# Summing products over states on TensorE: two half sums in two tiles instead of one whole sum every second tile

## What is computed

```
def step(h, inp):
    u_t, dt_t, B_t, C_t = inp
    h = jnp.exp(dt_t[..., None] * A) * h + (dt_t * u_t)[..., None] * B_t[:, :, None, :]
    y = jnp.einsum('bkdn,bkn->bkd', h, C_t)
    return (h, y)
```

## Time and profile before

| | |
|---|---|
| median of 3 runs | 13085.13 us |
| profiled execution, its own time | 13084.96 us |
| its span | 13082.8 us |
| mean granted TensorE clock | 0.697 of full speed |
| TensorE (PE) matmuls | 9361.0 us, 72% |
| VectorE (DVE) | 10128.2 us, 77% |
| GpSimd (POOL) | 9739.9 us, 74% |
| ScalarE (ACT) | 7120.1 us, 54% |

### The profile page before, as it was taken

One profiled execution on the slowest core, in us unless ns is written; L12 is line 12 of the kernel. 1 busy time (PEld: TensorE's weight loads), 2 busy tenths in 40 slices (PEclk: granted clock), 3 DMA queues, 4 the chain that ended last, 5 costly groups with the idle time before them and its releaser, 6 DMA issues.

```text
span 13082.8 us, 94515 instructions
## 1 busy us (share of the span) xinstructions
PE 9361.0 (72%) x26432; PEld 2316.8 (18%) x26432; DVE 10128.2 (77%) x5979; ACT 7120.1 (54%) x10802; POOL 9739.9 (74%) x4231
## 2 busy tenths in 40 slices
PE   5866688766886677768777778876678667776665
PEld 1211122111221112212122112211112111221121
DVE  2899967897689978888788876889778997888600
ACT  3655545554465545766466754655446554676324
POOL 1888867887688877877778776789768887788600
PEclk8955578756785567768777777865679557776665
DMA  3656676566655555545664657656665555555410
GB/s 77 142 130 128 129 129 130 134 128 130 134 139 132 126 142 137 123 121 129 148 136 118 122 135 132 135 130 128 132 132 137 129 128 147 131 128 124 100 47 15
DMA packets 1762968, 1627.25 MB, mean 124 GB/s; under 512 B 1304446, under 2 KB 1305760, under 8 KB 1762444
## 3 DMA queue, kind: packets, MB, share of 16 engines
q1 hardware_dynamic: 1762444, 1621.22, 56.1%
HBM read 622.68 MB, written 192.94 MB: 62 GB/s over the span
## 4 chain that ended last, share of the span: by engine, by line
PE 29%; issue 21%; POOL 16%; DVE 16%; ACT 10%; DMA 5%; SPq 3%; DVEq 0%; POOLq 0%; ACTq 0%
POOL pr L1346 10%; DVE ps L1261 7%; DVE hs L1276 7%; PE ps L669 5%; PE ps L821 4%; PE ps L642 3%; POOL dur L1354 3%; PE ps L808 3%; PE ps L799 3%; PE ps L783 2%; ACT dec L1055 2%; POOL us L1337 2%; DMA sd<-y_d 2%; PE ps L686 2%; SPq L550 1%
## 5 line engine op out<-in xcount | busy, mean ns | idle before, releaser
L1346 POOL TENSOR_TENSOR pr<-hs,crep 128x1024 f32<-128x1024 f32 x3072 | 7187.8, 2351 | 2244.3 <-DVE hs L1276 1230.0
L1276 DVE TENSOR_TENSOR_SCAN hs<-dec,carry,ps 128x1024 f32<-128x1024 f32 x1728 | 4054.0, 2346 | 228.8 <-DVE ps L1261 5.4
L1261 DVE TENSOR_TENSOR ps<-ps,dur 128x1024 f32<-128x1024 f32 x2304 | 2794.2, 1213 | 1133.6 <-PE ps L808 927.5
L808 PE MATMUL ps<-sbc,selb 96*128 96x512 bf16 x4608 | 1929.3, 517 | 1754.0 <-DVE hs L1276 1248.3
L1055 ACT ACTIVATE dec<-dtr,ac 128x1024 f32<-128x1024 f32 x2304 | 2611.8, 1136 | 382.7 <-DVE hs L1276 374.6
L821 PE MATMUL ps<-pr,red 128*32 128x512 f32 x12288 | 2421.6, 873 | 105.3 <-POOL pr L1346 95.9
L1354 POOL TENSOR_TENSOR dur<-dur,brep 128x1024 f32<-128x1024 f32 x768 | 1806.0, 2352 | 135.9 <-DVE ps L1261 97.6
L1062 ACT ACTIVATE carry<-hs 128x1 f32<-128x1 f32 x2304 | 457.6, 199 | 2576.3 <-DVE hs L1276 2379.5
L1272 DVE TENSOR_TENSOR_SCAN hs<-ps,carry,dur 128x1024 f32<-128x1024 f32 x576 | 1337.1, 2335 | 264.9 <-POOL dur L1354 116.8
L1276 DVE TENSOR_TENSOR_SCAN hs<-dec,zero,ps 128x1024 f32<-128x1024 f32 x576 | 1351.6, 2346 | 75.4 <-DVE ps L1261 1.5
L642 PE MATMUL ps<-xb,tapw 96*96 96x512 f32 x2304 | 1200.8, 637 | 43.1 <-ACT sd L896 40.7
(11 more groups left out here) (117 smaller groups left out, 7018.1 us busy)
## 6 DMA issues: line engine op xcount, KB each, us to landing
dtr<-de SPq DMA_DIRECT2D x768, 512.0 KB, 7.7
dur<-us SPq DMA_DIRECT2D x768, 512.0 KB, 8.5
crep<-bc_d SPq DMA_DIRECT2D x512, 512.0 KB, 6.3
ust<-u_d SPq DMA_DIRECT2D x256, 384.0 KB, 5.1
y_d<-yst SPq DMA_DIRECT2D x768, 128.0 KB, 4.2
sd<-y_d SPq DMA_DIRECT2D x512, 192.0 KB, 4.6
brep<-bc_d SPq DMA_DIRECT2D x128, 512.0 KB, 7.5
u_d<-sd SPq DMA_DIRECT2D x64, 384.0 KB, 3.1
```

The lines of the kernel that those rows point to most:

```text
L808: mm = pe.matmul(ps[:, SLOT + 2 * (n % RS) + hf, :], selb[:, i % GT // 2, :], sbc[:, w % 2, B * hf:B * (hf + 1)], start=True, stop=True)
L1261: dve.tensor_tensor(slot(n), slot(n), dur[:, 2 * (G % 2) + i % 2, :], ALU.mult).then_inc(bu_v, 1)
L1276: dve.tensor_tensor_scan(hs[:, n % RH, :], dec[:, others(n) % RD, :], slot(n), init, ALU.mult, ALU.add).then_inc(scan_v, 1)
L1346: pool.tensor_tensor(pr[:, n % RP, :], hs[:, n % RH, :], crep[:, q, :], ALU.mult).then_inc(prod_g, 1)
```

## The change

The pair is the same, and so are the matmuls, their operands, strips and number. The half hf = 0 (strips 0 and 1) is now issued in iteration n = 2m+3, one tile earlier than before, and waits for the pair's products; the half hf = 1 (strips 2 and 3) in iteration n = 2m+4, where the whole pair stood before, and signals that the pair is summed. The wait for the collected bank goes with the first half.

```
-            def reduce2(m):
+            def reduce_half(m, hf):
                 w, r = divmod(m, NP)
                 g, q = divmod(r, NQ)
-                pe.wait_ge(prod_g, 2 * m + 2)
-                if q == 0:
-                    after(pe, ye_a, NG * w + g)
-                for hf in range(2):
-                    for j in range(2):
-                        strip = 2 * hf + j
-                        mm = pe.matmul(ps[32 * strip:32 * strip + 32, YB, :], red[:, :],
-                                       pr[:, (2 * m + j) % RP, B * hf:B * (hf + 1)], start=(q == 0), stop=(q == NQ - 1))
-                mm.then_inc(red_p, 1)
+                if hf == 0:
+                    pe.wait_ge(prod_g, 2 * m + 2)
+                    if q == 0:
+                        after(pe, ye_a, NG * w + g)
+                for j in range(2):
+                    strip = 2 * hf + j
+                    mm = pe.matmul(ps[32 * strip:32 * strip + 32, YB, :], red[:, :],
+                                   pr[:, (2 * m + j) % RP, B * hf:B * (hf + 1)], start=(q == 0), stop=(q == NQ - 1))
+                if hf == 1:
+                    mm.then_inc(red_p, 1)
...
-                    if i % 2 == 0 and n >= 4:
-                        reduce2((n - 4) // 2)
+                    if n >= 3:
+                        reduce_half((n - 3) // 2, (n - 3) % 2)
...
-            for m in range(W * NP - 2, W * NP):
-                reduce2(m)
+            for m in range(2 * (W * NP - 2) + 1, 2 * W * NP):
+                reduce_half(m // 2, m % 2)
```

## The result

The changed kernel takes **13291.57 us** (median of 4 runs, 13276.16 to 13303.08), the kernel before beside it 13082.11 us. The ratio is 1.0154, 95% interval 1.0133 to 1.0176: **1.5% slower, +209 us**. Forecast were 13302 us, +217 us. The size came out right, and half of its parts did not, as the stretches show.

What follows compares the result with a forecast made beforehand. No engine was full; VectorE's loop bounds stretches without side work, TensorE leads the chain in post. Terms 48 (no side work) + 73 (post) + 60 (convolution) + 36 (attention) = +217 us on 13085, 13302 us; range 12970 to 13650.

Steps and rivals of the forecast that it cites:

- A half costs what a whole burst does: Sums on TensorE: two strips take as long as four, so 1536 additional bursts cost 1521 to 2872 us of engine time.
- The figure carried on from the Trainium skill: Sums on TensorE: a straight line from the skill's 2.38 makes a half 0.81 of a whole, total about +65 us.
- TensorE's time by stretch: Windows with side work: TensorE busy 95.5 us in post, 83.2 in convolution, 76.7 in attention, at clocks 0.80, 0.93, 0.78.
- the 10300 that were named as a sign: Whole kernel: TensorE's busy time was to come out above 10300 us.
- No side work: hidden, as argued: Windows without side work: added burst covered by VectorE's 3.6 us in plain tiles; 1 us a window, +48 us.
- The 41 us against 32: Ten preparation tiles without side work: ten halves raise TensorE's work to 41 us against 32.3 us of VectorE.
- I cost this at nothing: First half's earlier wait for the copied bank: TensorE idles 0.75 us three times a window, covered by 0.8 us slack.
- GpSimd's products to be there before the fill is done: Plain tiles without side work: the later product is there before the fill is done, so the added burst is hidden.
- Charge the chain with the printed share of TensorE: Stretches with side work: added TensorE time times 48% in post (+73 us), 27% in convolution (+60), 18% in attention (+36).
- Rival 1: Stretches with side work: a fuller TensorE raises its clock and makes the kernel faster, 12980 us; chance 0.20.
- the 0.85 named as break-even: Post stretches: the granted clock, 76.4/90.1, at which the added bursts neither cost nor gain time.
- Rival 3: Preparation and earlier wait stall VectorE, clock doesn't rise: +7 us a window without side work, +736 in all, 13821 us; chance 0.15.

Runs made afterwards that it cites:

- Experiment 5: The change, but the first pair of each group stays whole in its even tile; 13134.95 us against 13071.85 for the kernel before, ratio 1.0045.
- experiment 1: The kernel before, with all pairs whole but issued one tile earlier; 13182.73 us against 13080.74, ratio 1.0078.
- experiment 6: The kernel before, with whole pairs one tile earlier except the first pair of each group, which keeps its even tile; 13087.46 us, ratio 1.0012.
- experiment 2: The kernel before, with each pair in two halves in its even tile, side work between them; 13168.54 us, ratio 1.0069.
- experiment 3: The change, with halves only for pairs 1 to 5, in the preparation tiles, and whole pairs elsewhere; 13107.99 us, ratio 1.0024 to the kernel before.
- experiment 9: The kernel before, plus two-strip bursts adding zero in odd tiles for pairs 1, 2, 3, 5 outside convolution; 13222.59 us against 13072.79, ratio 1.0111.
- experiment 10: The kernel before, with whole pairs 1, 2, 3 and 5 one tile earlier outside convolution, no burst added; 13038.35 us, ratio 0.9978.

## Why the prediction was right, and where not

- **A half costs what a whole burst does: right.** A four-instruction burst takes 1.05 and 1.92 us, an eight-instruction burst 1.07 and 1.94. From its start to the next matmul's, the half holds TensorE 0.98 us (2330.96 to 2331.94) and 1.85 us (2326.06 to 2327.91), the whole 0.99 and 1.87. L821 is busy 3911.7 us; forecast were about 4000. The figure carried on from the Trainium skill ("TensorE: Matmul & The Clock Gate", "Measured speedup vs the span model"), a half at 0.81 of a whole, is not what this chip does between two and four strips. Its +65 us falls with it. One reading behind the step was wrong, though: L799 is no burst of one strip. Its stationary operand is 96 columns wide (6*96), so that its 2.02 us compare a wide matmul with four narrow ones; only the halves themselves show the price of two strips.
- **TensorE's time by stretch: right.** Post 94.1 us a window ((16 x 98.5 + 12 x 88.3)/28) for 95.5; convolution 84.6 for 83.2; attention 73.3 for 76.7. Clocks 0.80 and 0.84, 0.92, 0.80 for 0.80, 0.93, 0.78. TensorE's busy time in all is 10105.3 us, less than the 10300 that were named as a sign: the sums take 1490 us more and TensorE as a whole only 744, since the rest of its work got shorter at the higher clock (a fill's matmul 466 ns on average instead of 517).
- **No side work: hidden, as argued; +2 us instead of +48.** The 41 us against 32 assumed the lower clock throughout; the stretch ran at 0.73 where it had 0.57.
- **"I cost this at nothing" is the step that failed.** The moved wait was read from one place in a stretch without side work, where ScalarE is on time. Beside the silu of the convolution, with its table loads, ScalarE is up to 4.6 us late. Experiment 5 puts the first pairs of the groups back and takes the loss from 209 to 63 us; part of that is their burst time. With no burst added (experiment 1 against 6) the place of the first pairs is worth 86 us. The prediction also took GpSimd's products to be there before the fill is done; TensorE's wait for them went from 96 to 423 us, 262 us of it in windows without side work, where nothing was lost. What the rest of it costs was not isolated.
- **"Charge the chain with the printed share of TensorE" came out wrong both ways, and only part of that is its own fault.** With convolution the change cost 4.9 us a window (136/28) where 2.1 were forecast, but the moved waits are in that: with the first pairs back the loss there falls from 136 to 62 us. The price of TensorE's time without the wait for the copy is, by the traces of experiments 5 and 2, 2.2 us for 6.3 us more a window and 2.4 for 7.9, so 0.35 and 0.30 of it, where 0.27 was charged; in experiment 3 it is 0.55 (2.3 for 4.2). So the share was somewhat low, by how much these runs don't fix. In post stretches it charged 0.48, and the zero bursts of experiment 9 cost 0.77 (4.4 us for 5.7 a window); yet the change, with as much TensorE time added, cost +32 us and not +73. Something came back there. It isn't GpSimd's wait for the sums: that fell in experiments 1, 6 and 10, which gain 40 to 64 us in post, but in the change it rose, in post windows from 653 to 780 us. The granted clock of the post windows rose from 0.73 to 0.82, with the zero bursts only to 0.74. No run separates the clock from the place of the first halves, so this part stays open.
- The total was near by luck, because these errors cancel: too much in post and without side work, nothing for the wait. **Rival 1** was right on the clock's direction and wrong on the sum: at 0.80 and 0.84 post stayed below the 0.85 named as break-even. **Rival 3** had the right wait in the wrong place.

## What to carry to other kernels

A burst of column strips is paid by its passes: splitting it doubles its price on TensorE, so split only where that engine has time to spare. Before moving an instruction one place up in an in-order queue, look up each semaphore that goes with it in the stretch where its releaser is latest, not where it is typical. An engine's share of the old chain is a weak price for an addition to it: here an added microsecond cost between 0.30 and 0.77 where 0.27 and 0.48 were charged. Where stretches have different limits, choose the order for each, which here turned +209 us into -95.

## What was not expected

The place of the sums matters beside their number: the same 1536 bursts, 9 pairs in 12 one tile earlier, shift post windows by -64 us, attention by +46 and convolution by +26 (experiment 6). Halves in four of twelve pairs outside convolution make the kernel faster by 71 us though they add 400 bursts at 0.37 us each by experiment 9; whole early pairs gain as much in post stretches, by shorter waits of GpSimd that the halves don't have. What the halves gain by there, and why they beat whole early pairs in attention stretches (-36 against +16 us), stays open.
